# A transformer block on one NeuronCore: two device programs joined into one, the projection's last output chunk packed by weight parts, the modulation's dot products placed at other tiles

## The reference

```python
mod = silu(c) @ ada_w.T + ada_b                        # six vectors of 576 per sequence
shift_msa, scale_msa, gate_msa, shift_mlp, scale_mlp, gate_mlp = split(mod, 6)
gate_msa, gate_mlp = tanh(gate_msa), tanh(gate_mlp)
h = rmsnorm(x, g1) * (1 + scale_msa) + shift_msa
q, k, v = split_heads(h @ qkv_w.T + qkv_b)
q, k = rmsnorm(q, qg) * 36 ** -0.5, rmsnorm(k, kg)
o = softmax(q @ k.T) @ v
x = x + gate_msa * (o @ proj_w.T + proj_b)
h2 = rmsnorm(x, g2) * (1 + scale_mlp) + shift_mlp
x = x + gate_mlp * (gelu_tanh(h2 @ fc1_w.T + fc1_b) @ fc2_w.T + fc2_b)
```

## Time and profile before

| | |
|---|---|
| median of 3 runs | 2937.92 us (2937.09 to 2938.67) |
| the profiled execution's own time | 2937.97 us |
| its span in the trace | 2936.2 us |
| first stage (to the barrier) | 0 to some 460 us |
| attention, then projection and MLP | 462 to 1886 us, then to the end |
| PE busy | 2891.7 us, 98% |

### The profile page before, as it was taken

How to read it: one execution, slowest core, us unless ns; L and a number is a source line. 1 busy time by engine, 2 the same in 40 slices (tenths; PEclk the granted TensorE clock), 3 DMA queues, 4 the chain that set the end, 5 groups by cost and what they waited for, 6 DMA issues and landing times.

```text
span 2936.2 us, 35353 instructions
## 1 busy us (share of the span) xinstructions
PE 2891.7 (98%) x13030; PEld 2183.2 (74%) x13030; DVE 1980.2 (67%) x2702; ACT 1578.8 (54%) x1921; POOL 208.6 (7%) x150
## 2 busy tenths in 40 slices
PE   7999997999999999999999999999999999999999
PEld 7999995666666666666666666788888888888887
DVE  6777767998988888888888887844343242424342
ACT  3433325767767767767767766634344343434342
POOL 1232310011000000000000000080000000000000
PEclk9999998999999999999999999999999999999999
DMA  6465554223223222223222223442222222322121
GB/s 225 138 202 169 175 172 133 76 60 86 77 73 88 76 62 84 77 73 87 77 64 81 76 74 97 125 133 87 73 85 73 81 78 80 102 89 85 41 68 50
DMA packets 238454, 282.67 MB, mean 96 GB/s; under 512 B 34960, under 2 KB 144016, under 8 KB 237392
## 3 DMA queue, kind: packets, MB, share of 16 engines
q1 hardware_dynamic: 233696, 271.33, 30.3%
q10 hardware_dynamic: 4592, 9.18, 0.9%
HBM read 195.50 MB, written 84.67 MB: 95 GB/s over the span
## 4 chain that ended last, share of the span: by engine, by line
PE 82%; DVE 1%; ACT 1%; issue 0%; ACTq 0%; DVEq 0%
PE ps L1500 16%; PE ps L1525 16%; PE ps L1585 15%; PE ps L1567 15%; PE ps L1512 14%; PE ps L1543 4%; PE ps L1511 2%; ACT gated L1207 1%; DVE x L1382 0%; DVE w_lo L1375 0%; DVE x L1385 0%; DVE x L1387 0%; ACT p_r L1151 0%; DVE tmp L1384 0%; PE ps L1555 0%
## 5 line engine op out<-in xcount | busy, mean ns | idle before, releaser
L1151 ACT ACTIVATE p_r<-ps 128x1024 f32<-128x1024 f32 x512 | 491.7, 1024 | 412.1 <-PE ps L1500 412.0
L1330 DVE TENSOR_TENSOR p_lo<-p_r,p_hi 128x1024 fp32r<-128x1024 f32 x512 | 612.8, 1217 | 0.0
L1500 PE MATMUL ps<-qT,kT 110*128 110x512 f32 x2048 | 573.2, 397 | 6.3 <-issue 6.0
L1500 PEld LDWEIGHTS ps<-qT,kT 110*128 110x128 f32 x2048 | 382.4, 189 | 140.5 <-issue 58.4
L1151 ACT ACTIVATE prob<-ps 128x1024 f32<-128x1024 f32 x512 | 483.4, 1030 | 1.0 <-PE ps L1500 0.5
L1511 PE MATMUL ps<-prob,vp 128*64 128x512 f32 x1024 | 453.1, 595 | 0.0
L1453 DVE TENSOR_TENSOR a_lo<-act,a_hi 128x512 fp32r<-128x512 f32 x144 | 102.7, 713 | 517.5 <-ACT a_hi L1194 517.5
L1512 PE MATMUL ps<-prob,vp 128*37 128x512 f32 x1024 | 451.7, 594 | 0.0
L1324 DVE CAST p_hi<-p_r 128x1024 fp32r<-128x1024 f32 x512 | 349.9, 693 | 135.0 <-ACT p_r L1151 133.6
L1585 PE MATMUL ps<-a_hi,w 128*128 128x512 f32 x1296 | 415.5, 393 | 0.6 <-DVE a_lo L1453 0.6
L1525 PE MATMUL ps<-p_hi,vx 128*128 128x512 f32 x1024 | 404.3, 395 | 0.1
(11 more groups left out here) (170 smaller groups left out, 3586.4 us busy)
## 6 DMA issues: line engine op xcount, KB each, us to landing
w_raw<-w SPq DMA_DIRECT2D x144, 320.0 KB, 2.9
qk_hi_scratch<-aw SPq DMA_DIRECT2D x32, 576.0 KB, 3.2
qk_lo_scratch<-aw SPq DMA_DIRECT2D x32, 576.0 KB, 4.4
kT<-qk_hi_scratch SPq DMA_DIRECT2D x128, 144.0 KB
qT<-qk_hi_scratch SPq DMA_DIRECT2D x128, 144.0 KB
v_scratch<-stv SPq DMA_DIRECT2D x32, 512.0 KB, 2.7
vp<-v_scratch SPq DMA_DIRECT2D x16, 1024.0 KB, 9.6
xb<-xT SPq DMA_DIRECT2D x8, 1280.0 KB, 10.7
```

Of the source, the lines that this page charges most:

```text
L1151: act.activation(out, ps[:, 2 * slot:2 * slot + 2, :].rearrange("p a b -> p (a b)"), ACT.Exp).then_inc(exp_done, 1)
L1330: dve.tensor_tensor(p_lo[:, j], p_r[:, j], f32(p_hi[:, q % HIGHS]), ALU.subtract).then_inc(plo_done, 1)
L1500: mm = pe.matmul(ps[:, 2 * (entry % RING) + h, :], kT[r][:, h, kt * P:(kt + 1) * P], qT[:, u % 2, h], start=True, stop=True)
```

## The change

It does the following, in the order of the program.

1. Both stages stand in one program; there is no barrier between them. The flag is loaded ahead of the last turn (PE), of the last low part (DVE) and of the last store (SP), and only the branch stays between the stages. PE may start the scores of steps 0 and 1 behind its last turn; step 2 waits for `tqlo_done`, the last low part, because that still reads its PSUM banks. POOL clears `osb` right after its last work in the first stage, and starts the memset of the second k buffer once the first score is made.
2. The first unit's loads are spread: behind the store of tile 28 the first k chunk and q, behind that of tile 29 v, behind that of tile 30 the other three k chunks.
3. At the front, the three late dots of the first vector go behind the square sums of tile 0, the gain constants go ahead of the first sum of squares (with their wait for `gain_ld`), and a `w_low` trades places with a `scaled`.
4. `DOTS` becomes `((0, 1), (2, 3), (), (4,))`, and the first block has its own row.
5. The projection's chunk m = 4 packs high and low weights as its two output halves: 9 matmuls for 14. Its sum is then taken across the halves on DVE, four instructions in `add_proj` where one was, in all 8 blocks. `add_proj(1, 4)` moves behind the first `a_lo`.
6. ACT touches the gelu's table with a 128x1 activation ahead of the wait for `o_comb`.

```diff
+    dve.wait_ge(gain_ld, 64)
+    dve.tensor_scalar(qscale[:], gain[:, 2:3], gain[:, 3:4], float(HD) ** 0.5, ALU.mult, ALU.mult).then_inc(gain_step, 1)
...
     dve.wait_ge(sq0_done, KC)
     sum_chunks(dve, 0)
-    dve.wait_ge(gain_ld, 64)
...
-    w_low(1, 0, wlo_done)
     dve.wait_ge(rb_mm, 1)
     scaled(0)
-    scaled(1)
+    w_low(1, 0, wlo_done)
     h0_low(0)
+    scaled(1)
     w_low(1, 1, wlo_done)
...
-    for m in range(2, KC):
-        shift(1, m, prod)
...
-    DOTS = ((0,), (), (1, 2), (3, 4))
+    DOTS = ((0, 1), (2, 3), (), (4,))
+    DOTS_FIRST = ((), (0, 1), (), (2, 3, 4))
...
+                if first and r == 0 and t == 0:
+                    for m in range(2, KC):
+                        shift(1, m, prod)
+                for m in (DOTS_FIRST if first and r == 0 else DOTS if more else DOTS_LAST)[t]:
                     dot(it, i, r, m)
```

```diff
-                first_unit.load(sp)
...
+            if last and r == 1 and t == 1:
+                first_unit.load_k(sp, 0)
+                first_unit.load_q(sp)
+            if last and r == 1 and t == 2:
+                first_unit.load_v(sp)
+            if last and r == 1 and t == 3:
+                for c in range(1, NIT):
+                    first_unit.load_k(sp, c)
...
+        pool.wait_ge(kones, 1)
         for j in range(2):
             pool.memset(osb[j][:], 0.0).then_inc(osb_zero, 1)
             pool.wait_ge(osb_zero, j + 1)
+        pool.wait_ge(s_mm, 1)
         pool.memset(f32(kT[1][96:PKW]), 1.0).then_inc(kones, 1)
...
+            pool.tensor_scalar(wp_hi[:, k, D:DP], f32(wp_lo[:, k, D:DP]), 1.0, None, ALU.mult).then_inc(wplo_done, 1)
...
+            if u == 0 and kt == 2:
+                pe.wait_ge(first_unit.tqlo_done, B * NT)
```

```diff
             if m < KF:
                 dve.tensor_tensor(x1[i % 2][:, m], x1[i % 2][:, m], gated[:, m % 2], ALU.add).then_inc(x1_done, 1)
+            else:
+                dve.tensor_copy(tmp[0:TL, KF], gated[TL:P, m % 2]).then_inc(halves_done, 1)
+                dve.tensor_copy(tmp[TL:P, KF], gated[0:TL, m % 2]).then_inc(halves_done, 1)
+                dve.wait_ge(halves_done, 3 * i + 2)
+                dve.tensor_tensor(tmp[:, KF], tmp[:, KF], gated[:, m % 2], ALU.add).then_inc(halves_done, 1)
+                dve.wait_ge(halves_done, 3 * i + 3)
+                dve.tensor_tensor(x1[i % 2][:, m], x1[i % 2][:, m], tmp[:, KF], ALU.add).then_inc(x1_done, 1)
...
+                parts = passes(k, wp_hi, wp_lo, o_hi, o_lo)
+                if m == KF:
+                    parts = ((wp_hi, o_hi), (wp_hi, o_lo)) if k < KF else ((wp_hi, o_hi),)
...
         proj_gate(1, 4)
+        act.activation(bound[:], gain[:, 0:1], ACT.Gelu_apprx_tanh)
         act.wait_ge(o_comb, 2 * NU)
```

More of the change, by code:

```diff
@@ new lines, in pool_part, with sums, body @@
+    def pool_part(pool):
+        pool.memset(ident[:], 0.0).then_inc(setup, 1)
+        pool.wait_ge(setup, 1)
+        pool.affine_select(out=ident[:], in_=ident[:], compare_op=ALU.not_equal, fill=1.0, base=0,
+                           pattern=[[-1, P]], channel_multiplier=1).then_inc(ident_done, 1)
+        pool.memset(f32(h_lo[0:2 * H, 1, 0]), 0.0).then_inc(zero_done, 1)
+        pool.wait_ge(zero_done, 1)
+        pool.memset(stv[:], 1.0).then_inc(vones, 1)
+        pool.wait_ge(vones, 1)
+        def sums(i):
+            pool.wait_ge(sq_done, i)
+            sum_chunks(pool, i)
+        pool.wait_ge(zero_dma, 16)
+        def body(it, first, last):
+            for r in range(B):
+                i = B * it + r
+                if not (last and r == 1):
+                    sums(i + 1)
+                    pool.wait_ge(hhi_done, i + 1)
+                    pool.tensor_tensor(h_lo[:, 1 - r], tmp[:, 0:KF], f32(h_hi[:, 1 - r, 0:KF]),
+                                       ALU.subtract).then_inc(hlo_done, KF)
+                    pool.wait_ge(hlo_done, KC * (i + 1) + KF)
+                    low(pool, h_hi[:, 1 - r], h_lo[:, 1 - r], tmp[:, KF], KF).then_inc(hlo_done, 1)
+        iterate(pool, NIT, body)
+        pool.wait_ge(hlo_done, KC * B * NIT)
+        pool.memset(f32(first_unit.kT[96:PKW]), 1.0).then_inc(first_unit.kones, 1)
@@ new lines, in norm_act, with affine, prep_act @@
+    def norm_act(act, i):
+        act.wait_ge(r_max, i + 1)
+        act.activation(rs[:], rs[:], ACT.Sqrt).then_inc(nrm_done, 1)
+    def affine(act, r, m):
+        act.activation(tmp[:, m], tmp[:, m], ACT.Identity, bias=mod[:, SHIFT_MSA, m, r:r + 1],
+                       scale=mod[:, SCALE_MSA, m, r:r + 1]).then_inc(aff_done, 1)
+    def prep_act(act, i, r, part):
+        if part == 0:
+            act.wait_ge(x_ld[r], 16 * (i // B + 1) if isinstance(i, int) else 8 * (i - r) + 16)
+            act.wait_ge(hlo_done, KC * i)
+            act.activation(tmp[:], xb[:, r], ACT.Square).then_inc(sq_done, 1)
+        elif part == 1:
+            norm_act(act, i)
+        elif part == 2:
+            act.wait_ge(xr_done, i + 1)
+            for m in range(KC):
+                affine(act, r, m)
+            act.wait_ge(aff_done, KC * (i + 1))
+            wait(act, qkv_mm, 2 * TPB * (i - 1))
+            act.activation(h_hi[:, r], tmp[:], ACT.Copy).then_inc(hhi_done, 1)
@@ L731 @@
+    return sync_part, pool_part, act_part, dve_part, pe_part
 RING = 3
@@ L1681 @@
     f2b[TL:, KF] = 0
+    pb = rows(n(L0_cond_proj_b))
+    pb[TL:, KF] = 0
     arrays = {
```

999 lines of the change are left out of this document (479 added, 520 removed).

## The result

| | before | after |
|---|---|---|
| median of 4 runs, us | 2937.59 (2937.09 to 2938.67) | 2911.80 (2911.07 to 2911.88) |
| ratio, 95% interval | | 0.9911 (0.9899 to 0.9923) |
| profiled execution, us (span) | 2937.97 (2936.2) | 2911.72 (2909.9) |

A forecast was written before the change was run, and what follows sets the result against it. PE, busy 98% of the span, was taken as the bound. Front 5.6, blocks 3.2, seam 7.7, projection 8.5 and gelu 0.3 sum to 25.3 us: 2937.9 to 2912.6 us, range 2905 to 2922.

The forecast's parts named there:

- Front: Start of the kernel: with the dots moved, tile 1 follows tile 0 at once; 7.05 less 1.4, 5.6 us won.
- the slip of the sums: Start of the kernel: gain constants ahead of the sum of squares wait for their loads; all behind moves by 0.7 us.
- The second slip: Start of the kernel: ACT gets the second `scaled` later; fourth weight piece and second half of tile 0 slip 0.7 us.
- Blocks: First stage's blocks: dots moved to t = 1 remove PE's waits; 3.8 less 0.6 in the seventh, 3.2 us won.
- Seam: Between first stage and attention: stores ahead of loads, no barrier, earlier last turn and first score; 7.7 us won.
- Projection: Output projection: five fewer matmuls in eight blocks, 9.15 us, less 0.6 lost in block 0; 8.5 us won.
- Gelu: Gelu's table load goes ahead of a wait, saving PE 0.6; the moved `add_proj(1, 4)` costs about 0.3; 0.3 us won.
- (a): Start of attention: k chunks land late behind the store of tile 30; 4.3 us lost and more, 2918; chance 0.10.
- (b): Projection: tail packing pays half, DVE's longer sum and ACT's late square hold PE; 9.15 becomes 4.5, 2916.6; chance 0.07.
- (c): Whole kernel: everything that can be won is won, 31.3 us, giving 2906.6; chance 0.12.
- (e): Front: dots as slow at their new place, tile 1 held up as before; 5.6 us lost, 2918; chance 0.05.
- (d): Blocks: dots overrun the 0.4 us slack at t = 1, PE stops and its clock falls; 37 us, 2953; chance 0.04.

The follow-up runs named there:

- run 7: Not a follow-up run: in "where it had run 7" it counts matmuls, 7 of the first half that PE ran at the low level in the kernel before.
- three_moves: Changed kernel with gain constants behind the low weights, GpSimd's first k-buffer memset after the third tile's scale in the seventh block, packed sum behind `split_w1`: 2907.69 us.
- seam_filled: Changed kernel with 30 matmuls of no use on PE, into a bank nobody reads, in the gap before the last turn: 2909.97 us.

## Why the prediction was right

The time was 0.8 us off. By its own steps:

- **Front, 5.6 forecast, 5.9 measured.** No wait at 45 us, 1.00 granted behind it, and the slip of the sums to 19.33 are shown; undoing the front cost 5.4 to 5.8. The second slip came near its size by luck. I had put it on the weights. They were late by 1.0 us: the low parts that the second half of tile 0 needs were done at 40.08 for 39.09 before. But PE did not wait for them; it began that half 0.8 us later still, since it ran 18 matmuls of the first half at the low level where it had run 7. The new order of the first pieces goes with this: in its ten traces PE waits 0.87 us inside the first tile and leaves the low level 6.4 to 9.1 us behind its first matmul, in the four with the old order 0.21 us and 3.4 to 5.5. The order was not changed by itself, so what it costs alone is open.
- **Blocks, 3.2 forecast, 4.7 measured.** The mechanism held, with its seventh block: one wait left, 1.58 us where I had forecast 1.8, on the two instructions named. The mis-sized term is the 3.8 us of the first six waits. I took a wait to cost what its row says; the steps from turn to turn were 0.72 to 1.07 us longer for rows of 0.56 to 0.92, 4.8 us, and 0.05 each behind them. What the row leaves out is the same for short and long waits, 0.15 to 0.16 us (1.16 us by the row lengthened its step by 1.32, 1.58 by 1.74). It fits how a row is counted: the row begins at the end of the last matmul, 0.36 us behind its start, while the next would have started 0.20 behind it. At the front I had counted so, 5.05 us for a row of 4.88, and in the blocks not. The seventh block then cost 0.4 where I had 0.6.
- **Seam, 7.7 forecast, 7.6 measured.** Shifted by what was won ahead of it (10.7 by measurement), my times were 439.1 for the last turn, 441.3 for the first score, 443.9 for the last low part and 446.1 for the end of the cast; they came at 439.12, 440.95, 443.86 and 446.06. Only the second chunk of k was 1.9 us later than I had it (446.2 for 444.3), which cost 0.3. What I did not see is that PE runs the whole seam at 0.50: I had copied durations of a stretch that was already slow, and so the sum stayed right while 1.8 us lay open. That forecast and measurement agree to 0.1 is luck in part: with the old seam, the way from the turn of tile 29 to unit 1 took 53.19, 53.77 and 54.68 us in three traces, so the seam's gain is 7.6 to 9.1 by the one that is taken.
- **Projection, 8.5 forecast, 8.2 measured.** Six steps from block to block fell from 132.03 to 130.90 us and the seventh chunk gave 1.12, 7.9 together where I had 1.15 each; the first chunk gave 0.3: unit 63 took 22.68 us for 21.98 before, 0.7 for my 0.6.
- **Gelu, +0.3 forecast, -0.2 measured.** Within its bounds, for the wrong reason. I priced the new place of `add_proj(1, 4)` as a cost of 0.3 against a gain of 0.6 from the table load. In fact a wait of 0.82 us for the low weights took the place of the 0.6 us. And I gave the packing 8.5 us as though the order belonged to another term: alone it pays 5.3, since its longer sum at the old place costs 2.3 us of wait and 1.6 of clock.

The misses have both signs (0.3 and 1.5 us too little, 0.1 and 0.8 too much), so the total misses by less than the blocks alone do.

Of the rivals, (a) came in small (0.3 of 4.3 us), (b) would have held for the packing without the new order, (c) and (e) did not occur, and (d) fell with the 0.4 us of slack holding: no new wait stands at the second tile of a block.

On the port that VectorE and GpSimd share, the rows above show which VectorE instructions a memset holds until it ends: a cast and a multiplication by constants (3.15 us for 0.23). A reciprocal beside its start (0.35 us) and a sum with one operand in PSUM (0.76 us) ran at their usual length. Beside GpSimd's subtraction the dot took 2.63 us for 0.75. The Trainium skill, page "SBUF — State Buffer", section "SBUF: two separate sides", has the shared pair as an exclusive lock held for a whole instruction, which a VectorE operation needs in its two-port mode, and with two inputs in SBUF only against a GpSimd operation that reads SBUF. This case's traces agree. The prediction had put the first kind as all operations with one source, which is too wide: the reciprocal has one source and was not held. It had priced the two places at 1.8 and 1.5 us; moving the memsets won 1.75 and 1.3.

## What to carry to other kernels

Price a wait of PE by the distance between two like instructions on either side of it, not by its row: each wait here cost some 0.16 us more than its row, whatever its length, and one that grew from 0.6 to 2.9 us cost 3.9 with the clock behind it. Where PE is late at the start, look at the distance between its matmuls' starts before you blame what feeds it. When a change makes a helper's work longer, look for the one place where something urgent is queued behind it on that engine; a saving spread over eight blocks can be half lost at one of them. A long GpSimd memset (3.5 us here) belongs where VectorE does two-source work or nothing, or where nobody waits for its casts, and its start should be tied to an event of VectorE's.

## What the hardware showed beyond expectation

- After 6.2 us of idleness PE's granted clock was 0.50 for 13.6 us of work with gaps (438.3 to 451.9), after 2.9 us for 3.4 us, after 1.58 us and less in a busy stretch not at all. The time at 0.50 differs between executions of the same code: in `three_moves`, whose seam is unchanged, it was 431.7 to 438.5 and again 442.0 to 448.8. Matmuls of no use in the gap brought 1.8 us.
- The granted clock that the views give for the first 38 us is no guide to the matmuls' speed: in the changed kernel's trace it reads 0.50 and in seam_filled's 1.00, and in both a pair of the first tile takes 0.92 us (0.56 later). What tells the level there is the distance between starts, 0.36 us before the change of level and 0.20 after it.
- The front varies from run to run. ScalarE could begin on the first x block between 15.0 and 16.5 us, and the turn of tile 0 came between 64.5 and 65.8 us in the four traces with the old front, between 58.8 and 59.9 in the seven with the new one. This sets what can be told from a single pair of traces.
